# Self edges of a graph attention moved into the node updates of their own layer, and one bias row of the dense stage added by TensorE

## What is computed

```python
h = relu(layernorm(x));  agg = segment_sum(edge_attr_128, dst)           # edge sums
x = x + layernorm(relu(relu([h, agg] @ W1 + b1) @ W2 + b2) @ W3 + b3) * ln_w + ln_b   # dense stage
x0 = x;  x = relu(layernorm(x))
src, dst = [edges, loops]                  # every node also has an edge to itself
for l in range(2):                         # two attention layers
    q, k, v = projections of layernorm(x), its position term and the degree term   # 8 heads of 16
    att = clip(sum(q[dst] * k[src]) / scale, -50, 50), NaN -> 0
    ex = exp(att);  s = segment_sum(ex, dst)
    x = x + (segment_sum(ex * v[src], dst) / (s + 1e-16)) @ Wo + bo
    x = x + gelu(layernorm(x) @ W1 + b1) @ W2 + b2
return x0 + x                              # the kernel's output
```

## Time and profile before

| | us |
|---|---|
| median of 3 runs | 3553.08 |
| lowest and highest run | 3547.33 and 3558.46 |
| profiled execution, first to last instruction (span) | 2632.1 |
| median of the runs less that span | 921.0 |
| mean granted TensorE clock, share of 2.4 GHz | 0.931 |

### The profile page before, as it was taken

How to read it: one execution, slowest core, us unless ns; L and a number is a source line. 1 busy time by engine, 2 the same in 40 slices (tenths; PEclk the granted TensorE clock), 3 DMA queues, 4 the chain that set the end, 5 groups by cost and what they waited for, 6 DMA issues and landing times.

```text
span 2632.1 us, 60679 instructions
## 1 busy us (share of the span) xinstructions
PE 2104.4 (80%) x13853; PEld 1757.0 (67%) x13854; DVE 1978.7 (75%) x7060; ACT 1766.3 (67%) x4889; POOL 1805.2 (69%) x1967
## 2 busy tenths in 40 slices
PE   6989978766788888888888876677788778778877
PEld 6988943355677677676677755566666666666766
DVE  6898958756788888888888865677777777776775
ACT  6766756465677677677677735567677777777763
POOL 5746445477777777777777726777777777777773
PEclk9999989789999999999998887999999999999998
DMA  7867723233344434434444413333343333333332
GB/s 213 263 210 223 223 81 122 94 104 106 114 117 121 123 115 121 122 116 122 120 116 121 121 56 102 106 110 114 110 115 114 109 114 113 109 114 113 110 113 62
DMA packets 187155, 327.00 MB, mean 124 GB/s; under 512 B 38950, under 2 KB 100963, under 8 KB 186864
## 3 DMA queue, kind: packets, MB, share of 16 engines
q0 software_dynamic: 80208, 216.22, 28.6%
q1 hardware_dynamic: 105632, 106.77, 13.1%
q10 hardware_dynamic: 1024, 1.06, 0.1%
HBM read 291.56 MB, written 20.71 MB: 119 GB/s over the span
## 4 chain that ended last, share of the span: by engine, by line
POOL 46%; issue 21%; PE 17%; DVE 9%; DMA 3%; ACT 2%; DVEq 2%; POOLq 1%; ACTq 0%; SPq 0%
POOL arena L2131 44%; PE bank L1121 7%; DMA arena<-kv_rows,idx_stage 3%; PE bank L2222 2%; PE bank L1126 1%; DVE aggregate L2270 1%; PE bank L1856 1%; DVE arena L2278 1%; PE bank L2213 1%; PE bank L1850 1%; POOL norm_stat L1402 1%; DVE bn L1569 1%; DVEq L2259 1%; ACT arena L1507 1%; PE bank L1446 1%
## 5 line engine op out<-in xcount | busy, mean ns | idle before, releaser
L2131 POOL DMA_INDIRECT arena<-kv_rows,idx_stage x1612 | 1525.4, 946 | 552.0 <-issue 489.3
L2222 PE MATMUL bank<-arena 128*128 128x136 f32 x3328 | 602.5, 315 | 231.7 <-DVE aggregate L2270 225.4
L2222 PEld LDWEIGHTS bank<-arena 128*128 128x128 f32 x3328 | 486.4, 206 | 336.6 <-DVE aggregate L2270 241.3
L2213 PE MATMUL bank<-queries,arena 128*128 x3328 | 496.1, 296 | 182.0 <-DVE arena L2291 143.5
L2213 PEld LDWEIGHTS bank<-queries,arena 128*128 128x128 f32 x3328 | 439.7, 205 | 237.6 <-issue 235.3
L2270 DVE TENSOR_TENSOR aggregate<-bank,aggregate 128x136 f32 x1664 | 492.9, 296 | 122.5 <-PE bank L2222 49.6
L2291 DVE TENSOR_TENSOR arena<-bank,arena 128x512 f32<-128x512 f32 x416 | 286.8, 690 | 363.5 <-DMA arena<-kv_rows,idx_stage 294.9
L2152 ACT ACTIVATE arena<-iota_n,at_negdst 128x128 f32<-128x128 f32 x1664 | 527.8, 395 | 2.9 <-DMA queries<-arena 1.8
L2163 ACT ACTIVATE arena<-bank 128x512 f32<-128x512 f32 x416 | 247.2, 594 | 209.7 <-PE bank L2198 192.0
L2278 DVE TENSOR_TENSOR arena<-arena,bank 128x512 f32<-128x512 f32 x416 | 282.4, 679 | 20.3 <-ACT arena L2179 20.3
L2198 PE MATMUL bank<-ident,arena 128*128 128x128 f32 x1664 | 271.2, 289 | 19.0 <-ACT arena L2157 19.0
(11 more groups left out here) (336 smaller groups left out, 2768.8 us busy)
## 6 DMA issues: line engine op xcount, KB each, us to landing
arena<-in_edge_attr_dram SPq DMA_DIRECT2D x244, 256.0 KB, 3.5
arena<-kv_rows,idx_stage POOLq DMA_INDIRECT x1612
kv_rows<-arena SPq DMA_DIRECT2D x12, 512.0 KB, 3.8
kv_rows<-arena SPq DMA_DIRECT2D x24, 256.0 KB, 2.1
queries<-in_x_dram SPq DMA_DIRECT2D x13, 256.0 KB, 3.8
arena<-in_x_dram SPq DMA_DIRECT2D x12, 256.0 KB, 4.0
x_rows<-arena SPq DMA_DIRECT2D x12, 256.0 KB, 2.9
x_stream<-arena SPq DMA_DIRECT2D x12, 256.0 KB, 2.3
```

Source lines behind the costliest of these rows:

```text
L2131: pool.indirect_dma_start(kv[:, n, :], None, kv_dram[l], bass.IndirectOffsetOnAxis(idx_stage[:, half % 2, n:n + 1], 0)).then_inc(Z.kv_in[s ...
L2213: m = pe.matmul(bank[:, ATT_BANK[1][r % 2], j * D:(j + 1) * D], sel_t[:, r % SELT_SLOTS, j, :], q_all[:, bass.ds(tiles[j], 1), :].rearrang ...
L2222: pe.matmul(sums_of(j), sel[:, r % SEL_SLOTS, j, :], msg[:, r % 2, j, :], start=True, stop=True).then_inc(Z.sum, 1)
```

## The change

Self edges: the dense stage and the slots 14 and 15 of layer 0 lose them. In both layers a pair's update now begins with slot 0 ("own"): SP loads the k and v rows of the pair's own nodes from DRAM into new buffers (256 KB for a pair), DVE forms logits (`prod`, `logit`, `clip`, `att` in slot 0), ACT the exponential, DVE the weighted v (`message`) and its sum with `agg` (`total`) in slot 1. The weights' sum takes the self edge in `guard`. `agg` is cleared once it has been read: by ACT in the dense stage, by DVE (`clear`) in layer 0. The three last tiles do the part before `total` in quads 4 and 5 of the first body (`AHEAD_SLOTS`).

Bias row: PE writes b3 into the PSUM bank by a product of a row of ones with the bias row (`row_ahead`), and the third product accumulates onto it. DVE's statistics k=1 and ACT's normalisation k=1 read the bank itself, and DVE's addition (L1622) is gone.

```diff
@@ sp_update
+                if r == SLOT["own"] and u.own:
+                    if u.again:
+                        sp.wait_ge(*u_before(u).done("dve", "message"))
+                        sp.sem_inc(Z.turn, 1)
+                    sp.dma_start(u["own"], u.rows(kv_dram[l])).then_inc(update_move["own", u.b], 16)
+                if not u.nodes_too:
+                    return
@@ pe_dense
-                                     start=True, stop=True)
+                                     start=False, stop=True, skip_group_check=True)
+            def row_ahead(u, side, row):
+                pe.matmul(bank[:, 2 * u.b + side, 0:u.cols], ones_f[0:1, :], row.unsqueeze(1).to_broadcast([1, u.t, D]), start=True, stop=True)
...
                     transposes(e, z, 1)
                 if c:
+                    row_ahead(c, 0, rows_0[0:1, 0, :])
                     pe.wait_ge(*done("act", "h2_sb", c))
@@ act_dense
-                    normalise(c, 1, xob, z)
+                    normalise(c, 1, bank[:, 2 * c.b, 0:c.cols].rearrange("p (t d) -> p t d", d=D), z)
...
+                    act.activation(a.nodes(agg), ones_f[:, 0:1].unsqueeze(1).to_broadcast([P, a.t, D]), ACT.Copy, scale=0.0
+                                   ).then_inc(unit_sem("act", a), 1)
...
-                elif e:
-                    exp(e)
@@ dve_dense
                     dve.wait_ge(*done("pe", "o", c))
-                    count(c, dve.tensor_tensor(xob[c.b][:, 0:c.t, :], from_bank(c), rows_0[:, 0:1, :].to_broadcast([P, c.t, D]), ALU.add))
-                    dve.wait_ge(*done("dve", "o", c))
-                    stats(c, 1, xob)
+                    stats(c, 1, from_bank(c))
...
-                    loop_logits(e)
-                    if not a and not final_unit(e):
-                        held.append(e)
-                    else:
-                        loop_messages(e)
@@ slots of the node updates
-               "qkv0": (14, 0), "qkv1": (14, 1), "prod": (14, 2), "logit": (14, 3), "clip": (14, 4), "att": (14, 5),
-               "weights": (15, 0), "self": (15, 1)}
+        GAP = {"prod": (0, 3), "logit": (0, 4), "clip": (0, 5), "att": (0, 6), "message": (1, 3), "total": (1, 6),
...
+               "qkv0": (14, 0), "qkv1": (14, 1)}
@@ act_update
+                if r == SLOT["exp"] and u.own:
+                    act.wait_ge(*u.done("dve", "att"))
+                    act.activation(u.atts(5), u.atts(2), ACT.Exp).then_inc(own_exp[u.b], 1)
@@ dve_update
+                if at == GAP["prod"]:
+                    dve.wait_ge(*u.moved("own"))
+                    if u.again:
+                        dve.sem_inc(Z.turn, 1)
+                    count(u, dve.tensor_tensor(u["ownm"], u.nodes(q_all), u["own"][:, :, 0:D], ALU.mult), 0)
...
+                if at == GAP["message"]:
+                    dve.wait_ge(*u.weighed())
+                    count(u, dve.tensor_tensor(heads(u["ownm"]), heads(u["own"][:, :, D:2 * D]), per_head(u.atts(5), u), ALU.mult), 0)
...
+                if at == GAP["total"]:
+                    dve.wait_ge(*u.done("dve", "message"))
...
+                    count(u, dve.tensor_tensor(u["z"], u.nodes(agg), u["ownm"], ALU.add), 0)
                 if at == GAP["guard"]:
-                    count(u, dve.tensor_scalar(u.atts(3).rearrange("p (t h) -> p t h", h=HEADS), u.nodes(agg, D, MW), SUM_GUARD, None, ALU.add), 0)
+                    count(u, dve.scalar_tensor_tensor(out=u.atts(3).rearrange("p (t h) -> p t h", h=HEADS), in0=u.nodes(agg, D, MW),
+                                                      scalar=SUM_GUARD, in1=u.atts(5).rearrange("p (t h) -> p t h", h=HEADS),
+                                                      op0=ALU.add, op1=ALU.add), 0)
...
+                    if at == GAP["clear"]:
+                        dve.tensor_scalar(u.nodes(agg, 0, MW), ones_f[:, 0:1].unsqueeze(1).to_broadcast([P, u.t, MW]), 0.0, None, ALU.mult)
```

More of the change, by code:

```diff
@@ L1268, in each @@
             return tuple(f"{name}{k}" for k in range(n))
-        SELF = ("prod", "logit", "number", "clip", "att", "self")
+        OWN = ("prod", "logit", "number", "clip", "att", "message", "total")
         def steps_of(who, t):
@@ L1506, in normalise @@
                 for t in range(u.t):
-                    last = act.activation(dest[u.b][:, t, :], rows[u.b][:, t, :], func, bias=shift[:, t:t + 1], scale=factor[:, t:t + 1])
+                    last = act.activation(dest[u.b][:, t, :], rows[:, t, :], func, bias=shift[:, t:t + 1], scale=factor[:, t:t + 1])
                 last.then_inc(unit_sem("act", u), 1)
-            def exp(u):
-                act.wait_ge(*done("dve", "att", u))
-                act.activation(u.nodes(agg, D, MW), att_s[u.b][:, 2, 0:u.t * HEADS].rearrange("p (t h) -> p t h", h=HEADS),
-                               ACT.Exp).then_inc(unit_sem("act", u), 1)
             def free(u):
@@ L1531, in mlp_step @@
                     move(e, 1, t_sb[e.b])
-                while held:
-                    exp(held.pop())
                 if a and not first_unit(a):
-                    normalise(a, 0, xb, z, ACT.Relu)
+                    normalise(a, 0, xb[a.b], z, ACT.Relu)
                     free(a)
                 if d:
-                    normalise(d, 2, xo, xob, ACT.Relu)
+                    normalise(d, 2, xo[d.b], xob, ACT.Relu)
                 if a and not first_unit(a):
@@ L1551, in mlp_step @@
                     act.dma_start(e.nodes(q_all), qkv[e.b][:, 0:e.t, 0:D]).then_inc(move_sem["out", e.b], 16)
-                if e and not a and not final_unit(e):
-                    held.append(e)
-                elif e:
-                    exp(e)
             return mlp_step
@@ L1568, in stats @@
                 for t in range(u.t):
-                    last = dve.bn_stats(bn[u.b][:, t, :], rows[u.b][:, t, :])
+                    last = dve.bn_stats(bn[u.b][:, t, :], rows[:, t, :])
                 count(u, last)
@@ L1682, in gnn_kernel, with __init__ @@
         update_move = {(name, b): sem(f"update_{name}{b}") for name in UPDATE_TRANSFERS for b in SETS}
+        own_exp = sems("own_exp", len(SETS))
         class Updated:
-            def __init__(self, l, j, base, b=0):
+            def __init__(self, l, j, base, b=0, ahead=False):
                 self.l, self.j, self.base, self.b = l, j, base, b
+                self.own, self.nodes_too = ahead or b == 0, not ahead
                 self.t = UPDATE_TILES[b]
@@ L1772, in __call__ @@
                 begins, ends = counted or newest >= 0, counted or newest > 0
+                if not counted and i == 0 and h == 0 and r in AHEAD_SLOTS:
+                    base = self.load(FULL - 1, 1)[0]
+                    for u in (Updated(self.l, 0, base, 1, True), Updated(self.l, 0, NT - 1, 2, True)):
+                        self.stages(AHEAD_SLOTS.index(r), u, *gap)
                 if r == 0 and gap in ((), (self.loads_at,)):
```

99 lines of the change are left out of this document (38 added, 61 removed).

## The result

The change takes 3576.72 us (median of 8 runs, 3568.16 to 3590.05) where the kernel before takes 3548.16 in the same comparison (8 runs, 3538.14 to 3565.96): a ratio of 1.0083, 95% interval 1.0061 to 1.0105. That is 0.8% slower, more than the 0.3% that can be told from no change, and outside the predicted range. The prediction of 3539 us was wrong in sign.

The account below looks back on a forecast made before the run. POOL's gathers were taken to bound the layers, a ring of waits the dense stage. Dense stage -12, layer 0's drain -1.7 and -0.4, `total` +0.1 gave -14 from 3553.08: 3539 us, range 3528 to 3557.

Parts of the forecast that it names:

- 921.0 us outside the span as fixed: Whole kernel: the median's excess over the traced span of 2632.1 us was taken as unaffected by the change.
- whatever the change does to DVE inside the layers costs and gains nothing while DVE keeps up: Both attention layers: POOL's gathers, 1.25 us each, set the time, so DVE's work there counts 0.
- +0.6, with all register work +0.9: Layer 0: us of DVE work added per pair, within 2.1 us of waiting for gathered rows, so cost 0.
- Rival 2: Layer 0: DVE becomes the bound, waiting for its own rows' load; +29 us, 3582 us, chance 0.07.
- the prediction's 0: Layer 1: all the self-edge work, about 2.1 us a pair or 52 us of DVE, costs nothing.
- Dense stage, -12: Dense stage: steps -9, first two steps -1, drain -1.5, the end -0.5 us.
- seven fast and three slow ones: Dense stage: of ten steps, seven at 12.1 us and three at 13.2, 124.3 us against 133.35, so -9.
- the ring: Dense stage: cycle of waits between engines, 13.47 us round; removing self edges shortens POOL's shift there by 0.46 us a step.
- The bias row: Dense step: dropping DVE's addition saves 0.73 us, PE's row product costs 0.65 at full or 0.95 at low clock.
- POOL and the clearing: Layer 0: DVE's clearing of `agg` does not hold up POOL's gathers, 0; upper bound +7 us.
- The own loads: Layers: SP's loads of a pair's own rows land in 4.0 us; in layer 0 about 9 us of cover hides them.
- The drain of layer 0, -1.7 - 0.4: End of layer 0: -1.7 us from DVE's self edges gone, -0.4 from ACT's last DMA going out earlier.

Follow-up runs that it names:

- before_third: The kernel before, unchanged, traced once more in a comparison with TensorE stops (before 3495.27 us): 3491.99 us.
- kind A: Comparisons on chips where the unchanged kernel before takes some 2640 us, without the TensorE stops: 2641.3 and 2638.22 us.
- after_fifth: The change, unchanged, against the kernel before (2638.22 us) in the last comparison: 2656.27 us, ratio 1.0062.
- own_only: The change with the dense edit taken back (DVE adds the bias row; self edges moved), against the kernel before: 2644.85 us, ratio 1.0020.
- before_again: The kernel before, unchanged, with a trace of its own: 2642.04 us, where before in the same comparison takes 2641.3.
- kind B: Comparisons on chips where the kernel before shows TensorE stops, the first result's included: before takes 3548.16, 3495.27, 3540.49 and 3499.01 us.
- best_second: The change with own exponential before the Gelu chunks, clearing on ACT and no dense edit, against the kernel before: 2624.75 us, ratio 0.9952.

## Why the prediction was wrong

*"921.0 us outside the span as fixed."* The first step that failed. The trace and the times beside it came from executions of unlike kind; 1.7 to 1.8 us lie outside a span in every execution traced here. By that premise the layers ran at POOL's rate in the timed runs, and "whatever the change does to DVE inside the layers costs and gains nothing while DVE keeps up". In the runs that were timed DVE had fallen behind already: in before_third as in the change it is 25 to 51 us behind the gathers once a dozen quads of layer 0 are done, 36 in the median. But this alone doesn't make the sign, since the change is slower by 0.6% in kind A as well.

*Layer 0.* The step that failed in sign: "+0.6, with all register work +0.9" a pair against 2.1 us of slack, "so it still keeps up: 0". The work was sized about right: `total` 0.43, the clearing 0.32, less the copy of 0.18. The price left out was a wait. I had followed DVE's wait for the own load, which shows in no trace, and took the exponential as ready, without asking what stands ahead of it in ACT's slot. It was 2.6 us a pair. With 0.6 of work that is 3.2 against 2.1: over 24 pairs 26 us. The 27.7 of after_fifth lie close to it by luck. own_only has the same work and the same wait in its layers and lost 12.4, and DVE fell behind only from about the 80th of the 208 quads on, for the slack isn't even: before_again waits for gathered rows for 42 us from 540 to 700, 25 from 700 to 860, and then 9, 7 and 4 in each 160 us. Why the two traces differ by 15 us stays open; the dense edit, which only after_fifth has, doesn't touch the layers' code, and the statistics' wait for ACT's copy is 29.7 us in after_fifth and 19.5 in own_only.

Rival 2 had the mechanism and its threshold ("from 2.1 us of new work and waiting for a pair"), with the wrong wait and a chance of 0.07, and stood outside the range. That its result (+29, 3582) lies next to the 3577 measured is luck too: it was worked out for layers at POOL's rate, which the timed runs didn't have. In layer 1 2.1 us of work and the same wait fit in kind A: 1008.1 us where before_again takes 1009.5, as the prediction's 0 says.

*Dense stage, -12.* The size was near, the working not. From the first sum for x1 to the first gather the change takes 9.6 us less in kind A, and 8.3 to 10.9 less than before_third in kind B. Its steps at clock 1.00 take 11.7 to 11.8 us where 12.1 were forecast, but the second takes 16.6; that ten steps together came to 123.5 us, where 124.3 were forecast from seven fast and three slow ones, is luck. Removing the self edges does it all (own_only -13.8). I had put their share on the ring at 0.46 us a step; it was 0.8 between steps at full clock (12.7 to 11.9), and 1.6 against the steps at 0.87 (13.5), because the clock no longer falls. The bias row, for which I had most of the gain, is a loss by itself. In the change it saves 0.1 us a step and tends to cost the second step: 13.5 to 16.6 us in nine traces with it, 12.9 to 13.4 in four without (self edges out in all). The Trainium skill (TensorE: Matmul & The Clock Gate, "Part 1: The HAM clock gate") says that activity releases the throttle. What I drew from it, that the row product's extra work holds the clock, these rows don't bear out: with the row product and the self edges TensorE was busy for 10.50 of 12.60 us and the clock fell in the next step, with neither it was busy for 9.52 of 11.89 and the clock held.

*POOL and the clearing*: 0 was right. Of the 19 gathers that ran beside a clearing (L2050) in after_fifth, 17 took 942 to 947 ns and the longest 1071, so the hold-up that the Trainium skill allows for (SBUF — State Buffer, "Who interferes with whom") hardly shows. *The own loads*: hidden, right; the product that waits for them (L2006) has no idle time before it in after_fifth. *The drain of layer 0, -1.7 - 0.4*: lost in the backlog; in best_second, without backlog, it gave 0.5 (51.9 for 52.4).

## What to carry to other kernels

When an operation that hangs on another engine is moved, look up what stands ahead of its partner in that engine's own order at the new place, table loads included: with the stops, the wait for an operation of 0.2 us cost 32 to 36 us in three comparisons, more than the whole loss of the change, and putting the operation ahead of its neighbour gave it back. Slack read from a trace has to hold work and waits together, and a backlog that buffers swallow comes due where the stage drains. Slack isn't even over a stage, either, so a mean over 300 us doesn't give the price. And where the span of a trace and the times beside it differ by a quarter, the trace isn't one of the timed executions: a kernel that should win in both must not live on slack that only one of them has.

## What the runs showed of the hardware

In some comparisons and not in others, TensorE stands for 4.8 us on average (17 at most), 163 to 183 times in each of the twelve executions of kind B that were traced, in the stop that was looked at with products issued and their semaphores not yet raised: the same kernel takes 2638 to 2641 or 3495 to 3548 us. The granted clock is 1.00 in that stop, and 0.77 to 0.79 in the mean from the first to the last gather, where kind A has 0.93 to 0.95. The dense stage, in which TensorE is about as busy as in the layers (80%), is free of the stops in both (153.2 and 154.5 us from the first to the last sum for x1). What sets them off is open.
